# A decoder block in float32 on one core: weights staged in another order, the last transposes in idle banks, one output-projection tile per step

## What is computed

```python
x = x + attn(layernorm(x), q_w, q_b, k_w, k_b, v_w, v_b, o_w, o_b)   # causal, 16 heads
x = x + mha(layernorm(x), ctx_2048, ctx_2048)                        # causal, 16 heads
n = layernorm(x)
logits = n @ W_gate.T                                                # 8 experts
rw = softmax(top_k(logits, 2))
x = x + relu(n @ W_up.T) @ W_down.T + sum(rw) * (n @ W_expert)
```

## Time and profile before

| | |
|---|---|
| median of 3 runs | 745.69 us (744.91 to 746.27) |
| profiled execution, its own time | 742.88 us |
| its span, first to last instruction | 740.8 us |
| mean granted TensorE clock, as a share of 2.4 GHz | 0.986 |
| PE busy | 679.4 us (92%), 4480 matmuls |
| DVE busy | 499.9 us (67%) |
| ACT busy | 504.7 us (68%) |
| POOL busy | 256.7 us (35%) |

### The profile page before, as it was taken

One profiled execution on the slowest core, in us unless ns is written; L12 is line 12 of the kernel. 1 busy time (PEld: TensorE's weight loads), 2 busy tenths in 40 slices (PEclk: granted clock), 3 DMA queues, 4 the chain that ended last, 5 costly groups with the idle time before them and its releaser, 6 DMA issues.

```text
span 740.8 us, 13857 instructions
## 1 busy us (share of the span) xinstructions
PE 679.4 (92%) x4480; PEld 525.6 (71%) x4480; DVE 499.9 (67%) x1726; ACT 504.7 (68%) x1450; POOL 256.7 (35%) x390
## 2 busy tenths in 40 slices
PE   4998999989999999899868967999989999999798
PEld 3776787767777777677656745777768776777586
DVE  6667676665766676666868785767896669664522
ACT  6678877667777678787888874776687657773110
POOL 3745554424464346622553516511221112000100
PEclk9999999999999999999999997999999999999899
DMA  9653523346331563446846593444364443510101
GB/s 318 166 143 87 134 64 73 87 113 186 86 85 44 150 189 83 100 107 188 212 115 172 121 286 85 100 100 107 73 174 98 115 99 94 143 36 1 57 1 57
DMA packets 52330, 86.12 MB, mean 116 GB/s; under 512 B 8612, under 2 KB 16804, under 8 KB 52260
## 3 DMA queue, kind: packets, MB, share of 16 engines
q1 hardware_dynamic: 52256, 85.25, 44.1%
HBM read 27.55 MB, written 7.34 MB: 47 GB/s over the span
## 4 chain that ended last, share of the span: by engine, by line
PE 77%; DVE 8%; ACT 6%; POOL 4%; issue 2%; DMA 1%; SPq 1%; POOLq 0%; DVEq 0%
PE m L511 15%; PE t L472 14%; PE m L512 14%; PE m L513 14%; PE pv L505 9%; PE s L457 8%; DVE probs L657 3%; ACT probs L877 2%; PE m L472 2%; POOL probs L989 1%; DVE prob L667 1%; ACT prob L886 1%; PE m L526 1%; DVE xT_lo L741 1%; ACT xT_hi L912 1%
## 5 line engine op out<-in xcount | busy, mean ns | idle before, releaser
L657 DVE CUSTOM_DVE_ANT_0 probs<-s,mask 128x128 f32<-128x128 f32 (+3 forms) x512 | 246.6, 483 | 137.3 <-PE s L457 134.6
L877 ACT ACTIVATE probs<-probs,negmax 128x128 f32<-128x128 f32 (+3 forms) x512 | 284.4, 558 | 50.9 <-DVE negmax L657 48.2
L457 PE MATMUL s<-stack 96*128 96x128 f32 (+3 forms) x512 | 199.0, 395 | 11.1 <-DVE negmax L657 7.8
L472 PE MATMUL t<-ident,probs 128*128 128x128 f32 x1105 | 196.8, 276 | 4.3 <-POOL probs L989 2.6
L989 POOL TENSOR_SCALAR probs<-probs,rsum 128x128 f32<-128x128 f32 (+3 forms) x256 | 133.2, 539 | 190.8 <-DVE rsum L671 190.8
L886 ACT ACTIVATE prob<-t 128x384 f32<-128x384 f32 (+1 forms) x226 | 121.1, 536 | 109.3 <-PE t L472 109.3
L472 PEld LDWEIGHTS t<-ident,probs 128*128 128x128 f32 x1105 | 140.5, 141 | 50.0 <-issue 5.9
L457 PEld LDWEIGHTS s<-stack 96*128 96x128 f32 x512 | 97.8, 191 | 24.7 <-issue 8.7
L667 DVE COPY prob<-t 128x128 f32<-128x128 f32 (+1 forms) x221 | 76.6, 347 | 35.0 <-PE t L472 33.9
L877 ACT ACTIVATION_READ_ACCUMULATOR probs<-probs,negmax 128x1 f32 x512 | 98.4, 192 | 0.0
L511 PE MATMUL m<-xT_hi,w_lo 128*128 128x512 f32 x192 | 78.5, 409 | 1.5 <-DVE xT_lo L723 0.9
(11 more groups left out here) (136 smaller groups left out, 1005.3 us busy)
## 6 DMA issues: line engine op xcount, KB each, us to landing
stack<-stage SPq DMA_DIRECT2D x384, 128.0 KB, 2.3
xt<-in_x SPq DMA_DIRECT2D x16, 256.0 KB, 4.1
xres<-in_x SPq DMA_DIRECT2D x4, 1024.0 KB, 5.9
kraw<-in_ctxT SPq DMA_DIRECT2D x16, 256.0 KB, 3.3
cv<-in_ctx SPq DMA_DIRECT2D x16, 256.0 KB, 3.1
x<-xres SPq DMA_DIRECT2D x3, 1024.0 KB, 4.6
res<-x SPq DMA_DIRECT2D x8, 256.0 KB, 6.5
out<-res SPq DMA_DIRECT2D x2, 1024.0 KB, 4.8
```

The source lines that it names most:

```text
L457: nc.tensor.matmul(score_tile(P, i), stack[0:RS, P % 2, h, 0, chunk(qb)], stack[0:RS, P % 2, h, 1, 0:N], start=True, stop=True).then_inc(s ...
L472: mm = nc.tensor.transpose(dst[:, chunk(qb - kb)], probs[:, (2 * P + h) % 3, OFF[qb] + PART * kb:OFF[qb] + PART * kb + PART], ident[:, :])
L657: nc.vector.tensor_tensor_reduce(probs[:, (2 * P + h) % 3, OFF[qb]:OFF[qb + 1]], score_tile(P, i), mask[:, T - N:T], -SCALE, BIG, ALU.add, ...
L877: nc.scalar.activation(tile, tile, ACT.Exp, bias=negmax[:, P % 2, h, qb:qb + 1], scale=-1.0, accum_out=total).then_inc(p_exp, 1)
```

## The change

`FEED` moves the feeds of batches 2 and 3 by four slots, half a step. The output projections of the last two self batches are put at one tile per step: O(2,3) goes from step 29 to step 31 and O(3,3) from step 39 to step 40, and the store of `x2[2]`, the reload of `xres` and its bias move with them by three steps. The statistics and norms of j = 5 and 6 move (j = 5: steps 32 and 33 to 34 and 35; j = 6: steps 41 and 42 to 43), their `ln_scale` with them. All three feed-forward weights pass through `V[1]`, in the order UP, EXPERT, DOWN, split at steps 38 and 39, 42 and 43, 45 and 46; `f_norm(0)` waits for the last output projection. The transpositions of the last feed no longer go through the two `m` banks one after another: `turn_last` does them tile by tile into the banks s0, s1, s2 and t0, which no pair uses by then. In steps from 64 on, `back` stands one slot earlier.

```diff
-FEED = tuple(PAIRS * (PAIRS * (f + B + 1) + 2) + 4 for f in range(B))
+FEED = tuple(PAIRS * (PAIRS * (f + B + 1) + 2) + 4 + 4 * (f // 2) for f in range(B))
...
     if j == B + 2:
-        return [z + 14, z + 15, z + 20, z + 21]
-    return [z + 1, z + 5, z + 9, z + 13] if j == B + 1 else [z - 7, z - 3, z + 1, z + 5]
+        return [z + 24, z + 25, z + 28, z + 29]
+    return [z + 17, z + 20, z + 24, z + 25] if j == B + 1 else [z - 7, z - 3, z + 1, z + 5]
...
+    if j <= B + 2:
+        return [z + 32, z + 33, z + 36, z + 37]
     return [z + 28, z + 29, z + 32, z + 33]
...
             if b == B - 1:
-                put(("O", b, t), SELF_END + min(t, 2), 4 * (t // 3), 4)
+                put(("O", b, t), SELF_END + t, 0, 4)
             elif b == B - 2:
-                put(("O", b, t), (25, 28, 29, 29)[t], 4 * (t // 3), 4)
+                put(("O", b, t), (25, 28, 29, 31)[t], 4 * (t // 3), 4)
...
+            if f < B - 1:
+                put(("FL", f, m), 0, u + 1 + 2 * m, 1)
...
+    for m in range(KC):
+        key = ("FL", B - 1, m)
+        bank_of[key] = 3 + m
+        ended.setdefault(feed_start(B - 1) + 2 + m, []).append(key)
...
-        f_raw = {UP: f_xln, EXPERT: V[1], DOWN: V[1]}
+        f_raw = {UP: V[1], EXPERT: V[1], DOWN: V[1]}
...
+                for n in range(1, B):
+                    first = PAIRS * n + 5 if n < B - 1 else NPS + 1
+                    if s == first:
+                        sp.wait_ge(o_out, NT * n)
+                        sp.dma_start(x2[n - 1], xres[:, :, :]).then_inc(x2_stored[n - 1], 16)
+                    if s == first + 1:
+                        sp.wait_ge(x2_stored[n - 1], 16)
+                        sp.dma_start(xres[:, :, :], x_in[n]).then_inc(res_loaded, 16)
...
                 if s == SELF_END:
                     sp.wait_ge(pv_done, NT * (SELF_AT[-1] + 1))
+                    load_weight("upT", UP)
+                if s == SELF_END + 3:
+                    sp.wait_ge(f_lo_done, KC)
                     load_weight("expert", EXPERT)
-                if s == SELF_END + 3:
+                if s == SELF_END + 4:
                     sp.wait_ge(o_mm, NT * B)
-                    load_weight("upT", UP)
                     sp.wait_ge(x2_stored[2], 16)
                     load_x(res2, x2[2])
-                if s == SELF_END + 3:
-                    sp.wait_ge(f_lo_done, KC)
+                if s == SELF_END + 6:
+                    sp.wait_ge(f_lo_done, 2 * KC)
                     load_weight("downT", DOWN)
...
+            def turn_last():
+                f = B - 1
+                for t in range(NT):
+                    pe.wait_ge(f_ln, NT * f + t + 1)
+                    for m in range(KC):
+                        dst = out_bank(("FL", f, m))
+                        mm = nc.tensor.transpose(dst[:, chunk(t)], f_xln[:, t, chunk(m)], ident[:, :])
+                        if t == NT - 1:
+                            mm.then_inc(fl_mm, 1)
...
+                    if z == feed_start(B - 1) + 1:
+                        turn_last()
...
-                    if s % 2 == 0 and other(s // 2 - 1) and i == 4:
+                    if s % 2 == 0 and other(s // 2 - 1) and i == (4 if s < NP else 3):
                         back(s // 2 - 1)
...
                     if f == 0:
-                        dve.wait_ge(f_lo_done, 2 * KC)
+                        dve.wait_ge(o_mm, NT * B)
...
-                    if s == stats_slots(j)[-1] // PAIRS + 1:
+                    if s == stats_slots(j)[-1] // PAIRS + (j not in (B + 1, B + 2)):
                         ln_scale(j)
...
-                    if s == NPS + t // 2:
+                    if s == NPS + 3 + t // 2:
                         biased(B - 1, t)
...
-                for n, slot in enumerate((EXPERT, UP, DOWN)):
+                for n, slot in enumerate((UP, EXPERT, DOWN)):
                     for c in range(KC):
-                        if s == SELF_END + 1 + ((0, 1, 1, 1), (3, 3, 4, 4), (5, 5, 6, 6))[n][c]:
+                        if s == SELF_END + 1 + ((0, 1, 1, 1), (4, 4, 5, 5), (7, 7, 8, 8))[n][c]:
                             f_split(n, slot, c)
```

More of the change, by code:

```diff
@@ L162, in plan @@
         for m in range(KC):
-            put(("FL", f, m), 0, u + 1 + 2 * m, 1)
+            if f < B - 1:
+                put(("FL", f, m), 0, u + 1 + 2 * m, 1)
             put(("FU", f, m), 0, u + UP_AT + 4 * m, 4)
@@ L349, in out_bank @@
         def out_bank(key):
-            return [*m_bank, pv_bank][BANK_OF[key]]
+            return [*m_bank, pv_bank, *s_bank, *t_bank][BANK_OF[key]]
         def chunk(c):
@@ L409, in _ @@
                     sp.dma_start(xres[:, :, :], x_in[0]).then_inc(res_loaded, 16)
-                if p == 5 + b // 3 and 1 <= b < B:
-                    sp.wait_ge(o_out, NT * b)
-                    sp.dma_start(x2[b - 1], xres[:, :, :]).then_inc(x2_stored[b - 1], 16)
-                if p == 6 + b // 3 and 1 <= b < B:
-                    sp.wait_ge(x2_stored[b - 1], 16)
-                    sp.dma_start(xres[:, :, :], x_in[b]).then_inc(res_loaded, 16)
+                for n in range(1, B):
[6 more added lines that the diff above has]
+                        sp.dma_start(xres[:, :, :], x_in[n]).then_inc(res_loaded, 16)
                 if s == 20:
@@ L418, in _ @@
                     load_x(xt, x2[0])
-                if s == 30:
+                if s == 32:
                     sp.wait_ge(o_mm, NT * 3)
@@ L579, in fill @@
                     if n == 0 and m == 0:
-                        pe.wait_ge(f_lo_done, KC + c + 1)
+                        pe.wait_ge(f_lo_done, c + 1)
                     mm = three(dst, (w_hi[:, UP, c, chunk(m)], w_lo[:, UP, c, chunk(m)]), (xT_hi[:, c, :], xT_lo[:, c, :]), c)
@@ L585, in fill @@
                     if n == 0 and m == 0:
-                        pe.wait_ge(f_lo_done, c + 1)
+                        pe.wait_ge(f_lo_done, KC + c + 1)
                     mm = three(dst, (xT_hi[:, c, chunk(m)], xT_lo[:, c, chunk(m)]),
@@ L852, in _ @@
                         c_recip(s // 2 - 1)
-                    if s % 2 == 0 and other(s // 2 - 1) and i == 5:
+                    if s % 2 == 0 and other(s // 2 - 1) and i == (5 if s < NP else 4):
                         back_scaled(s // 2 - 1)
```

## The result

| | before | the change |
|---|---|---|
| median of the runs | 745.65 us (744.91 to 746.27, 4 runs) | 736.36 us (734.54 to 738.57, 4 runs) |
| profiled execution, its own time (span) | 742.88 us (740.8) | 738.57 us (736.6) |
| ratio of the times | | 0.9877, 95% interval 0.9848 to 0.9906 |

9.3 us less, where 15.2 were forecast. The change was measured twice more beside the experiments: 732.76 us (ratio 0.9836, 0.9817 to 0.9856) and 735.22 us (0.9858, 0.9834 to 0.9882). The profiled execution above is the slowest of its four, that of before was 2.8 us faster than its median; so the two spans differ by 4.2 us only, and stages say more than ends.

The account below looks back on a forecast made before the run. TensorE (PE), busy 679.4 of 740.8 us, was taken to set the pace nearly everywhere. Terms from -9.4 (restaging) and -6.4 (tail) to +1.7 summed to -15.2, moving the median 745.69 to 730.5 us; range 725 to 736.

Parts of the forecast that it names:

- Restaging: Step 42: f_norm(0) starts at 444.0 instead of 453.40, -9.4 us; the stretch to the next step shortens, -0.8.
- The collision: Step 42: f_norm(0) meets POOL's EXPERT splits, up to 0.88 us more for each norm, +1.5 (bounds 0 and 2.6).
- Statistics in step 43: Step 43: four blocks of 0.82 us land on DVE, +1.7 us (bounds 0.9 and 4.2).
- SP holding DOWN's load and the stack of pair 46: Steps 43 to 45: SP holds both behind the EXPERT splits, but the stack is needed only at step 45; costed at nothing.
- Output projections: Steps 39 to 41: one tile per step, -2.36 + 1.20 and an eviction of 0.6, -0.6; steps 29 and 31: 0.
- Batch 1's norm and the clock: Around steps 35 and 36: shorter wait for probabilities -1.3, clock kept -1.0, norms crowding into step 36 +0.4.
- The statistics that left steps 32 and 33: Steps 32 and 33: four statistics leave the thin steps, -0.6 us (0 to 3.3).
- The tail: Last feed: later feeds cover PE's wait and transposes use idle banks, -6.4; thin stretch in steps 58 to 60, +1.3.
- Rival 1: DVE becomes the bound of steps 41 to 45; collisions +1.1, step 43 +2.5, clock +1.0, thin stretch +1.5: 736.6; chance 0.20.
- Rivals 2, 3 and 4: 2: everything good, 726.0, chance 0.12; 3: clock stays low before feed 2, 785, 0.03; 4: f_norm(0) wait stays, 740.7, 0.03.
- The signs: Step 42: no w_lo wait, 9 to 11 us; step 43 past 10; wait before pair 35 about 1.6; last transposes unwaited.
- sign of being wrong: Step 42 still holds a wait over 3 us, or steps 58 to 60 give back more than 3 us.

Follow-up runs that it names:

- e4: The change with DOWN's load issued one SP step later, behind the stack of pair 46, measured again: 731.41 us, ratio 0.9813 to the kernel before.
- e2: The change with GpSimd's scale of batch 2's cross norm behind the last two EXPERT splits: 731.56 us, ratio 0.983 to the kernel before.
- e1: The change with DOWN's load issued one SP step later, behind the stack of pair 46: 732.89 us, ratio 0.9829 to the kernel before.
- f3: Every fix in one kernel, measured again: e2 with batch 3's residual one SP step later and all EXPERT splits in step 43: 729.24 us, ratio 0.9776.
- r1: The kernel before with the restaging of the weights alone: 738.41 us, ratio 0.9903 to the kernel before.
- e3: e2 with all four EXPERT splits in step 43, none beside f_norm(0): 731.03 us, ratio 0.9807 to the kernel before.
- a0: The changed kernel itself, measured a second time: 732.76 us, ratio 0.9836 to the kernel before.
- a1: The changed kernel itself, measured a third time: 735.22 us, ratio 0.9858 to the kernel before.
- t1: The kernel before with the tail's part of the change alone: 740.11 us, ratio 0.9936 to the kernel before.
- t3: e2 with feeds 2 and 3 at their old slots, last transposes still in the idle banks: 732.54 us, ratio 0.9823 to the kernel before.
- d1: The change with one more unused 1 MB transfer behind DOWN's load and ahead of the stack of pair 46: 735.47 us, ratio 0.9862 to the kernel before.

## Why the prediction was right or wrong

**The direction and most terms held; one place, which I had costed at nothing, took 1.9 to 6.2 us in the profiles.** With that place mended the kernel takes 731.4 to 732.9 us (e4, e2, e1), near the 730.5 that were forecast. The change itself measured 5.9, 2.3 and 4.7 us above the forecast; at the end, side by side, the stall was worth 3.8 us (e4), so that it doesn't account for all of the first miss.

- *Restaging.* `f_norm(0)` lost its wait for `w_lo` and started right behind the scale, as written. Steps 41 and 42 gave 6.4, 6.8 and 6.1 us in the three profiles, where -9.4 - 0.8 + 1.5 = -8.7 stood. What is missing is mostly the clock, by an estimate: I had step 42 at 9 to 11 us "at the full clock", and it ran at 0.78, which over 13.56 us is 3.0 us. In f3 (splits moved, clock 0.84) it takes 10.85. The 2 x 0.82 us for the two statistics have no support: r1 leaves them in place and gains 6.1 in the same steps.
- *The collision.* 1.03 and 1.37 against 0.53: 1.3 us, forecast 1.5. Its removal (e3) gave 1.7 in step 42 and took 2.6 in step 43.
- *Statistics in step 43.* +0.9, the low bound, forecast 1.7. Their real cost came by another way, next.
- *SP holding DOWN's load and the stack of pair 46: "I cost it at nothing".* **This step failed.** It measured +6.15, +1.86 and +3.25 us in steps 44 and 45 of the three profiles, and 0 in every kernel that undoes it (e1, e2, e4). I counted how much POOL has to do in step 43; I did not ask what the first thing in its queue waits for. POOL was busy for 0.23 us of that step, and its scale stood 10.22 us for a statistic that the same change had put late in that step. I also trusted the filled step 44 to cover the megabyte, and PE still waited.
- *Output projections.* Steps 39 and 40 gave 1.35, forecast 0.6: the eviction in step 41 cost nothing; that step fell from 9.64 to 7.11, as the stack wait of 3.14 at its end had gone. Steps 29 and 31: -0.15, forecast 0.
- *Batch 1's norm and the clock.* Forecast -1.3 - 1.0 + 0.4 = -1.9; steps 34 to 36 gave 1.7, 2.2 and 1.7. The wait ahead of pair 35's transposes fell from 2.94 to 1.64 us and step 35 kept the full clock (0.81 before), both as written; but a wait of 1.27 us for POOL's probabilities, at 387.93, is new, and step 35 gave 1.35 us (9.14 to 7.79). The statistics that left steps 32 and 33 gave nothing there, forecast -0.6. I overlooked that the change also moves batch 3's residual, 1 MB, to SP step 34, ahead of the stack of pair 37: PE waited 0.37 and 0.69 us for it in the change, and 1.6 in e4.
- *The tail.* Forecast -6.4 + 1.3 = -5.1. Steps 58 to 60 gave 1.4 and the rest 3.55, 4.95 in all (a0, a1); 4.6 with the tail alone (t1). The last stretch took 6.17, forecast 5.7 + 0.4. Right in size; but the shift of the feeds, to which I gave the cover, was not needed (t3).
- *The rivals.* Rival 1 stood at 736.6, and its time came out; its mechanism did not, as step 43 grew by its low bound and the missing time lay in steps 44 and 45. So that its time was met is luck (by the prediction's own bounds its last term is 1.4 and not 1.5, which makes it 736.5). Rivals 2, 3 and 4 fell.
- *The signs.* `f_norm(0)` without its wait, the scale just ahead of it, two of the four over 1 us, the wait of about 1.6 us, and the last transposes and the gate came out as written. Step 42 didn't (13.56 us at 0.78 for 9 to 11 at the full clock), nor did step 43, which stayed at 9.67 and below 10. Neither sign of being wrong came up; I had named none for steps 44 and 45.

From step 20 on, the three profiles of the change are 4.6, 12.9 and 10.4 us shorter than that of before; without what steps 44 and 45 lost they would be 10.7, 14.8 and 13.6 shorter, where the forecast says 15.2. The profile of before is itself 2.8 us below its median, so these differences are not those of the medians. The first profile of the change has three further stretches at the lower clock that a1's doesn't: in step 37 (+1.6 over a1), in step 45 (+2.9) and in step 60 (+1.6). Its four runs were granted 0.986 to 0.991 of the full clock, the four of a0 0.991 to 0.993; why can't be settled here.

## What to carry to other kernels

When a change puts a wait on a queue, price it by the latest release of everything queued ahead of the instruction that frees it, and look whether the same change has moved that release; the work of the engine in between says nothing. A late small transfer behind a large one needs both dates checked: when its issuer is free, and how long it takes to land, for the very load that the consumer waits for. Compare stages between profiles, not ends, where the part ahead of the change and the clock vary by more than the term in question.

## What the runs showed of the hardware

- The same standstill of PE has two prices. Waits of 2.97 (the change), 3.01 (a1) and 2.98 us (d1) at the same place were followed by a step at a mean clock of 0.75 (12.44 us) in the first, and by one at the full clock (9.50 and 9.51) in the two others. The Trainium skill's "TensorE: Matmul & The Clock Gate" (section "What's actually happening") has idling lower the clock. The traces agree in that PE had stood still before each drop named here; but a wait of one length was followed by a drop in one profile and by none in two, so its length alone doesn't decide it.
- The clock can fall without a long wait: in all three profiles of the change it fell at the start of step 42, in the first behind waits of 1.02, 0.62 and 0.26 us. The prediction had leaned on each low stretch following a standstill of about 3 us.
- A VectorE normalisation of 128x512 took 0.59 and 0.53 us in step 42 of the change, and 1.03 and 1.37 us where it met a subtraction of GpSimd's; with the splits moved away (e3) all four took 0.46 to 0.58.
- The part ahead of step 20, which no kernel here changes, ended between 242.7 (f3) and 245.7 us (a0), in the profiles, a spread of 3 us; times of single executions hold it too, so a difference of less than that between two of them says little.
